# A three-layer expert network with a convolution: interleaved rows behind the convolution, its bias folded into the next experts, and two experts split by batch instead of three

## The reference

```
x = x + experts0(gn(x))       # h = gelu(x w1[e] + b1[e]); out = h w2[e] + b2[e],  D=256, H=1024
x = x + conv3x3(gn(x)) + bias # 8 channels to 8, weights sign(w) * mean|w|, edge padding
x = x + experts2(gn(x))
x = x + experts3(gn(x))       # exact gelu in this one

def gn(v, G=4, eps=1e-05):    # groups of two channels, per batch
    m = mean(group); s = var(group)
    return (v - m) / sqrt(s + eps)
```

## Time and profile before

| | us |
|---|---|
| median of 3 runs (lowest to highest) | 613.98 (613.09 to 614.35) |
| the profiled execution | 614.43 |
| its span, first to last instruction | 612.4 |
| PE busy | 594.5, 97% of the span |
| ACT busy, DVE busy | 430.3 (70%), 423.2 (69%) |
| POOL busy | 31.3 (5%) |

### The profile page before, as it was taken

One profiled execution on the slowest core, in us unless ns is written; L12 is line 12 of the kernel. 1 busy time (PEld: TensorE's weight loads), 2 busy tenths in 40 slices (PEclk: granted clock), 3 DMA queues, 4 the chain that ended last, 5 costly groups with the idle time before them and its releaser, 6 DMA issues.

```text
span 612.4 us, 9520 instructions
## 1 busy us (share of the span) xinstructions
PE 594.5 (97%) x2973; PEld 501.0 (82%) x2973; DVE 423.2 (69%) x857; ACT 430.3 (70%) x741; POOL 31.3 (5%) x52
## 2 busy tenths in 40 slices
PE   7999999999999896999999999999999999999997
PEld 7778888888889775999888888888888888888885
DVE  4867968768787796767865866866775675675532
ACT  5766767677777685769867777777767777777743
POOL 2000000000000451000000000000000000000000
PEclk9999999999999997999999999999999999999999
DMA  8673355455363599801332323223234244234001
GB/s 273 188 238 105 113 163 176 119 165 152 108 178 103 197 116 110 177 2 63 109 105 77 130 68 118 88 74 133 70 109 132 86 123 136 86 116 142 17 19 69
DMA packets 56342, 72.80 MB, mean 119 GB/s; under 512 B 4064, under 2 KB 50160, under 8 KB 56304
## 3 DMA queue, kind: packets, MB, share of 16 engines
q1 hardware_dynamic: 56304, 72.33, 41.5%
HBM read 59.70 MB, written 8.42 MB: 111 GB/s over the span
## 4 chain that ended last, share of the span: by engine, by line
PE 87%; DVE 4%; DMA 2%; issue 2%; SPq 2%; POOL 1%; ACT 1%; DVEq 0%; POOLq 0%; ACTq 0%
PE G L1016 42%; PE ACC L1039 14%; PE ACC L1034 14%; PE ACC L1035 14%; DMA W2raw<-in_L_conv_w 1%; DVE Cl L894 1%; DMA XT<-XC 1%; PE TR L1052 1%; SPq L374 1%; DVE XC L903 1%; DVE BN L653 1%; SPq L436 1%; PE ACC L1122 1%; PE TR L982 1%; PE STAT L995 0%
## 5 line engine op out<-in xcount | busy, mean ns | idle before, releaser
L720 DVE TENSOR_TENSOR Hl<-HR,Hh 128x512 fp32r<-128x512 f32 (+1 forms) x216 | 136.2, 631 | 158.8 <-ACT Hh L563 157.5
L559 ACT ACTIVATE HR<-G,BT 128x512 f32<-128x512 f32 (+1 forms) x216 | 138.3, 640 | 137.1 <-PE G L1016 135.9
L1016 PE MATMUL G<-Xh,W1l 128*128 128x512 f32 (+1 forms) x432 | 163.9, 379 | 3.3 <-issue 1.9
L1016 PE MATMUL G<-Xl,W1h 128*128 128x512 f32 (+1 forms) x432 | 158.7, 367 | 0.0
L1016 PE MATMUL G<-Xh,W1h 128*128 128x512 f32 (+1 forms) x432 | 158.5, 367 | 0.0
L1034 PE MATMUL ACC<-Hh,W2l 128*128 128x512 f32 (+1 forms) x432 | 156.5, 367 | 0.0
L1035 PE MATMUL ACC<-Hh,W2h 128*128 128x512 f32 (+1 forms) x432 | 156.2, 366 | 0.0
L563 ACT ACTIVATE Hh<-HR 128x512 fp32r<-128x512 f32 (+1 forms) x216 | 126.3, 585 | 8.7
L1039 PE MATMUL ACC<-Hl,W2h 128*128 128x512 f32 (+1 forms) x432 | 123.5, 367 | 0.6 <-DVE Hl L720 0.6
L1016 PEld LDWEIGHTS G<-Xh,W1l 128*128 128x128 f32 x432 | 82.0, 190 | 16.1 <-issue 2.2
L1016 PEld LDWEIGHTS G<-Xh,W1h 128*128 128x128 f32 x432 | 81.9, 189 | 13.6
(11 more groups left out here) (73 smaller groups left out, 357.4 us busy)
## 6 DMA issues: line engine op xcount, KB each, us to landing
W1raw<-in_L_conv_w SPq DMA_DIRECT2D x24, 1024.0 KB, 5.1
W2raw<-in_L_conv_w SPq DMA_DIRECT2D x24, 1024.0 KB, 5.6
x_scratch<-XT SPq DMA_DIRECT2D x16, 256.0 KB
out_x<-OUTT SPq DMA_DIRECT2D x16, 256.0 KB, 2.2
XC<-x_scratch SPq DMA_DIRECT2D x16, 252.0 KB
XT<-XC SPq DMA_DIRECT2D x34, 112.0 KB
NAT<-in_x SPq DMA_DIRECT2D x6, 512.0 KB, 8.4
NAT<-in_x SPq DMA_DIRECT2D x4, 256.0 KB, 3.6
```

The costliest lines, as they stand in the source:

```text
L559: nc.scalar.activation(HR[:, t % 2, 0:n], G1[t % 2][:, 0:n], func, bias=BT[:, bass.ds(col, 1)]).then_inc(gelu_done, 1)
L720: nc.vector.tensor_tensor(Hl[:, t % RING, 0:n], HR[:, t % 2, 0:n], Hh[:, t % RING, 0:n].bitcast(F32), ALU.subtract).then_inc(hlo, 1)
L1016: ins = nc.tensor.matmul(G1[t % 2][:, 0:width(b)], w[:, ee, c, col], rhs, start=n == 0, stop=n == len(parts) - 1)
```

## The change

The program is written anew around a list of passes: `PASSES` holds every expert once, and experts 7 and 8 twice (one batch each). All engines walk the same flat list of units. What differs in the work:

- **Rows back.** Within each half of 128 features, feature d now lies on partition 2 (d mod 64) + (d div 64) for all of `XT` behind the convolution. `give_back` writes its rows two partitions apart, and blocks 4, 9, 13 now cross a border: 22 DMAs for a batch. W1 of the later layers is loaded in this order (two DMAs), W2's columns and the output's are put in order by the access patterns of ACT and DVE, and b2 is transposed in both orders.
- **Bias.** The convolution's mean is applied in DVE's addition, so ACT's step on line 622 is gone. The bias isn't added to x; it goes into the group means and shifts of the next layer and into b2 of its experts.
- **`load_xc`** is one DMA for one channel and batch instead of four, made possible by 11 copies of the last row in DRAM instead of one; `store_x1` writes them with one DMA for each batch.
- **Order.** Experts 7 and 8 are halved, 9 is whole, nothing is crossed. SP issues batch 0's 22 give-backs, then expert 9's weights, then batch 1's 22. The sums for expert 8 stand in DVE's program after tile 13 (batch 0) and in the fourth unit of expert 8, batch 0 (batch 1).
- **Buffers.** `CN`, `Ch`, `Cl` have four slots and POOL waits for matmuls instead of DVE; `HR` has four slots.

```diff
-HALVED = (C - 1, C, C + 1)
-CROSSED = (C, C + 1)
+HALVED = (C - 1, C)
+PASSES = [(E, bs) for E in range(EXPERTS) for bs in (((0,), (1,)) if E in HALVED else (BOTH,))]
...
+LAST = dict(evict=0, sums=1, aggregate=1, mean=3, eps=5, scale=6)
+FIRST = dict(sums=13, aggregate=13, mean=14, eps=15, scale=16, split=17)
...
+    (0, (0,), 0.5, {}),
+    (0, (1,), 0.5, dict(sums=unit(PC, 3), aggregate=unit(PC, 3), mean=unit(PC, 4), variance=unit(PC, 5),
+                        eps=unit(PC, 6), scale=unit(PC, 6))),
...
-                for j, nj, c, p0 in rows_back(k):
-                    sp.dma_start(XT[p0:p0 + nj, c, b].rearrange("p o n -> p (o n)"),
-                                 XC[j * C:(j + nj) * C, b, k, 1:N + 1]).then_inc(x2_in[b], 16)
+                    for j, n, c, g, i in rows_back(k):
+                        sp.dma_start(XT[GROUPS * i + g:GROUPS * (i + n):GROUPS, c, b].rearrange("p o n -> p (o n)"),
+                                     XC[j * C:(j + n) * C, b, k, 1:N + 1]).then_inc(x2_in[b], 16)
...
+            for q in range(TILES):
+                give_back(q)
+            load_w1(C + 1)
+            load_w2(C + 1)
+            for q in range(TILES, B * TILES):
+                give_back(q)
...
+            dve.wait_ge(bias_in, 16 * 2 * LAYERS)
+            nc.vector.tensor_copy(bias2_apart[:].rearrange("r (i g) -> r g i", g=GROUPS),
+                                  bias2_rows[:].rearrange("r (g i) -> r g i", g=GROUPS)).then_inc(bias_moved, 1)
...
+            pe.wait_ge(bias_moved, 1)
+            for i, rows in enumerate((bias2_rows, bias2_apart)):
+                at = LAYERS * C * HT + i * n
+                nc.tensor.transpose(TR[:, at:at + n], rows[:], ident[0:n, 0:n]).then_inc(bias_tr, 1)
             stay_busy(16)
```

More of the change, by code:

```diff
@@ L46, with pass_of, first_pass, last_pass @@
 NBLK = -(-D // OUTR)
-LASTROW = D + 2 - ROWS
+DP = OUTR * (NBLK - 1) + ROWS
 NP = N + 2
-DP = D + 2
 TILES = -(-NBLK // 2)
-CRING = 3
+CRING = 4
+BANKS = 3
+BOTH = tuple(range(B))
+HALVED = (C - 1, C)
+PASSES = [(E, bs) for E in range(EXPERTS) for bs in (((0,), (1,)) if E in HALVED else (BOTH,))]
+UNITS = HT * len(PASSES)
+def pass_of(E, b):
+    return next(p for p, (e, bs) in enumerate(PASSES) if e == E and b in bs)
+def first_pass(E):
+    return pass_of(E, 0)
+def last_pass(E):
+    return pass_of(E, B - 1)
@@ new lines, in unit, with halved, width, split_no @@
+def unit(p, t):
+    return HT * p + t
+def halved(p):
+    return len(PASSES[p][1]) == 1
+def width(p):
+    return N * len(PASSES[p][1])
+SPLITS = [(p, b) for p, (E, bs) in enumerate(PASSES) for b in bs]
+def split_no(p, b):
+    return SPLITS.index((p, b))
+def evicted_by(p):
+    return DC * (p + 1)
+PA, PB, PC, PD = (pass_of(E, b) for E in HALVED for b in range(B))
+def split_steps():
+    at = {}
+    for p, b in SPLITS[2:]:
+        if p == PD:
+            at[unit(PC, 7)] = (p, b)
+        elif p != PC:
+            at[unit(p - 1, 2 + 2 * b)] = (p, b)
+    return at
@@ new lines, in weight_steps @@
+def weight_steps():
+    at = {}
+    for E in range(1, EXPERTS):
+        p = first_pass(E) - 1
+        steps = [unit(p, t) for t in range(HT)]
+        if E in (C, C + 1):
+            steps = [unit(p - 1 + i, t) for i in range(2) for t in (1, 3, 5, 7)]
+        for k, u in enumerate(steps):
+            at.setdefault(u, []).append((E, k))
+    return at
+SPLIT_AT = split_steps()
+WEIGHTS_AT = weight_steps()
+LAST = dict(evict=0, sums=1, aggregate=1, mean=3, eps=5, scale=6)
+FIRST = dict(sums=13, aggregate=13, mean=14, eps=15, scale=16, split=17)
@@ new lines, with jobs_at, job_of @@
+NJOBS = len(JOBS)
+CONV_JOBS = {b: [J for J, (e, bs, of, _) in enumerate(JOBS) if of == 0 and b in bs] for b in range(B)}
+LAST_CONV_JOB = {b: max(CONV_JOBS[b]) for b in range(B)}
+LAST_JOB = LAST_CONV_JOB[B - 1]
+FIRST_JOB = LAST_JOB + 1
+def jobs_at(stage, u):
+    return [J for J, job in enumerate(JOBS) if job[3].get(stage) == u]
+def job_of(E, b):
+    f, e = divmod(E, C)
+    of = (-1, 0.5, 1)[f]
+    return next(J for J, job in enumerate(JOBS) if job[2] == of and job[0] == e - e % 2 and b in job[1])
```

1070 lines of the change are left out of this document (489 added, 581 removed).

## The result

| | us |
|---|---|
| predicted | 619.6 (611.0 to 627.0) |
| changed kernel, median of 4 runs | 634.73 (632.9 to 635.27) |
| kernel before, median of 4 runs beside them | 614.16 (613.09 to 615.74) |
| ratio, 95% interval | 1.0328 (1.0296 to 1.0359) |
| profiled execution, its span | 635.18, 633.4 |

A forecast was written before the change was run, and what follows sets the result against it. PE was taken to bound the kernel, busy 594.5 of 612.4 us. Parts 1 to 5 gave +4.2 us and part 6 +1.4, together +5.6, hence 619.6 us against the median, range 611.0 to 627.0.

The forecast's parts named there:

- What bounds the kernel: Whole kernel: PE bounds it, busy 594.5 of 612.4 us; the change leaves its work in whole and half units alone.
- Part 1, rows two apart: Give-backs: transfers become faster than their issue, so SP's issue sets the pace; 22 DMAs for a batch take 18.2 us.
- transfers aren't faster: Rival on give-backs: transfers stay at 1.0 us a piece, batch 1 ends near 260, total 629.6 us; chance 0.10.
- cheap issue: Rival on give-backs: at 0.6 us an issue, 22 take 13.2 us, both holes shrink, total 611.4 us; chance 0.20.
- Part 2, SP's start: Before the give-backs: `load_xc` saves 1.9 us, its store comes about 0.6 us later, first give-back at 210.3.
- Part 3, batch 0: Convolution: batch 0 complete at 230.5, PE hole of 6 us instead of 3.7, expert 8 starts at about 241.5.
- Part 4, batch 1: Expert 8: batch 1 lands at 250.2, its first unit starts at 259.5, and the wait costs 6.1 us.
- Part 5: From expert 8's batch 1 to expert 10: expert 9 starts at 271.8, expert 10's third unit at 298.8.
- Part 6, the start: Kernel start: first unit at 18.4 instead of 16.42 because of b2's copy; net +1.4 us, bounds 0.7 and 4.5.
- Parts at nothing: Priced at 0: ACT's missing step, W2's column orders, two W1 DMAs, small scale steps, extra rows stored, more copied code.

The follow-up runs named there:

- e5: The changed kernel with 480 bytes of padding, so that the hidden ring starts at 128 modulo 512 bytes: 625.88 us, ratio 1.0175.
- e4: The changed kernel with the 16 idle matmuls ahead of PE's wait for the spread bias rows instead of behind it: 630.87 us, ratio 1.0275.
- e15: The kernel before with only the rows two apart and matching W1, W2, b2 and output orders, ring at 128 modulo 512: 611.03 us, ratio 0.9942.
- e8: The changed kernel with the ring at 128 modulo 512 and the idle matmuls ahead of the bias wait: 623.96 us, ratio 1.0144.
- e10: e8 with the steps for the sums of expert 8, batch 0, two tiles later in the convolution: 623.71 us, ratio 1.0156.
- e12: e8 with each tile's second block given back by ACT's queue and batch 1's sums two half units earlier: 621.21 us, ratio 1.0105.
- e16: The kernel before with only the four split weight buffers moved to 256 modulo 512 bytes: 626.8 us, unit 2.817 us.

## Why the prediction was too low

- **What bounds the kernel**: right that PE does. Wrong was the sentence that the change "leaves PE's work in them alone". The pace of PE in whole units was the one thing not on the list of what changes, because no line of the diff is about it. Addresses change with every table that changes its size. This is the step that failed: that term was 0 without a reason given and measured 8.9 us in time (e5 against the changed kernel), most of the miss.
- **Part 1, rows two apart**: right in both halves. The transfers became faster than the issue, 22 issues took 18.78 us (forecast 18.2), and the landing came 1.7 us behind the last (2.2). The rival *transfers aren't faster* and that of the *cheap issue* are both refuted, by the DMA share and by 0.81 us a piece. (Two slips in the working, without effect here: the 40 issues of before took 34.1 us and not 33.8, and that first rival's 44 us of pieces and 10 us of weights end at 266 when they begin at 212, not near 260.)
- **Part 2, SP's start**: wrong in size. The first give-back began 22.5 us after half unit 64 (219.01 - 196.47), before 22.1, forecast 20.8. `load_xc` did lose its three DMAs, but the store ahead of it came 19.3 us after that unit instead of 16.9: not 0.6 later but 2.4. The forecast priced only the addition ahead of `evict`. In the trace PE's last `g2` of expert 7 now stands behind the six matmuls of the first tile (213.35 to 214.64, where before it ended 1.3 us ahead of that tile), and `evict` follows at 214.88.
- **Part 3, batch 0**: hole of 5.0 us in PE (6 forecast), right. From the landing to expert 8 it took 13.9 us instead of 11.0. The low clock took 3.4 us (4 x 0.46 + 4 x 0.39) instead of 2, and PE waited 1.6 us at 250.56 for a `Ch` that stands in ACT's queue behind `Xh`. The clock windows of the changed kernel:

```profile
240.00:244.00 4.00, 2.48 (x7) 2.10 (x8) 3.50 (x11) 0.00 (x0) 0.00 (x0) 0.54 0.95 348
244.00:248.00 4.00, 4.00 (x14) 3.24 (x13) 1.80 (x4) 0.00 (x0) 1.48 (x2) 0.61 0.99 250
```

- **Part 4, batch 1**: the mechanism stood: chain from landing to batch 1's first unit 9.7 us (269.64 - 259.91; forecast 9.3). It landed 9.7 us later than forecast because the first give-back was 8.7 late, 6.9 of that by the lag that PE already had at half unit 64. Expert 8 was late too, so PE waited only 2.7 us there, not 3 to 5.
- **Part 5**: 13.4 and 26.5 us (forecast 12.3 and 27.0). From half unit 64 to expert 10's third unit the loss was 8.0 us, of it 0.5 of pace; forecast 4.2.
- **Part 6, the start**: wrong in size. The first unit started at 22.59, not at 18.4. The idle matmuls began 1.9 us later than forecast, of it 1.5 by a wait for a piece of x, which varies from run to run (none before, 0.35 in e4), and lasted 2.3 us longer: what failed is the share for the clock, since the idle time of 2.8 us did drop it. Unit 8 was 4.8 us late, a little above even the upper bound of 4.5.
- **Parts at nothing**: W2's strided rounding takes 661 ns instead of 616 in whole units and shows nowhere (e15), so 0 was right. POOL was not on that list and did change. Its row answers to one of before with 827 ns:

```profile
L535 POOL TENSOR_SCALAR CN<-XC,CST 128x516 f32<-128x516 f32 x18 | 18.3, 1022 | 7.2 <-PE ACC L1026 3.6 <-issue 2.3 <-PE TR L1026 1.3
```

The Trainium skill, "SBUF — State Buffer", section "Who interferes with whom", says that a DVE instruction with two SBUF inputs contends with a POOL instruction that reads SBUF; `Cl` is one. Once POOL no longer waits for `Cl`, it runs beside it. The 1022 ns instead of 827 fit that, but no run separates it.

The sum: 8.9 of pace, 3.4 of the start (4.8 less 1.4) and 3.3 at the convolution (8.0 less 0.5 less 4.2) are 15.6; the miss was 15.1. The parts don't quite add, as e8 shows, because an earlier start is partly lost in the wait for batch 1. The direction doesn't hang on the addresses: e5, with the pace of before, is still 1.75% slower (0.7 to 2.8).

## What to carry to other kernels

Before a change is costed, compare where the buffers lie in SBUF: a table that grows by a few bytes moved every operand behind it, and cost 8.9 us, more than any step of the diff. Keep the moving operand and the weights of a matmul at the same start modulo 256 bytes: offsets of 32, 64 and 128 bytes cost here, 256 didn't. And when a transfer is made cheap, count its issues: here half of them on a second queue gave some 6 us, while steps moved in DVE's order gave nothing (e10) or cost 3.8 us (e12), and a matmul that is there to keep the clock up belongs ahead of a wait, not behind it.

## What the hardware showed unexpectedly

- Where moving operand and weights all start alike modulo 256 bytes, a matmul of 512 float32r columns took 390 ns by the profile (400 the first in a row) and a whole unit 2.751 us; where some don't, up to 397 (406) and 2.79 to 2.82 us, 1.5 to 2.4% of PE's time. Half units of 256 columns take 1.42 us in the changed kernel all the same. The Trainium skill, "SBUF — State Buffer", section "Who interferes with whom", calls PE's two read ports, for the moving operand and for weights, independent, and says that PE never waits on anyone. The runs here don't bear out that PE's two reads have nothing to do with each other: 2.817 us a unit in e16 instead of 2.751, with nothing changed but the start of the weights. Where the two meet, no run tells.
- The price of an issue on SP doesn't follow the bytes: 14 rows of 8 KB take 0.81 us (median of 44), the two W1 loads of 512 KB each 1.39 together, W2's 1 MB 0.59.
